# Attention between two quantised feed-forward blocks, one core: the reciprocal of the row sums moves ahead of other VectorE and GpSimd work, its spreading product one step later on TensorE

## The chip, the cores and the metric

The kernel runs on one core of a Trainium2 chip. The metric is the device time of one execution in microseconds. A core has TensorE (PE, matmuls, with its weight loads shown as PEld), VectorE (DVE), ScalarE (ACT), GpSimd (POOL) and SyncE (SP), which here only issues DMAs. Each engine works its own instruction list in order, and the lists meet in semaphores.

## The reference

```python
# x: (16, 512, 128); 16 heads of 64; all float32
x = x + 0.5 * ffn(layernorm(x))            # ffn: blockwise FP4-rounded inputs and weights, silu(gate) * up
x = x + attn(layernorm(x))
x = x + 0.5 * ffn(layernorm(x))

def attn(x):
    q, k, v = split_heads(x @ w_q), split_heads(x @ w_k), split_heads(x @ w_v)
    p = softmax(einsum('bnqd,bnkd->bnqk', q, k) * 64 ** -0.5)
    o = merge_heads(einsum('bnqk,bnkd->bnqd', p, v))
    y = o @ w_proj + b_proj + x
    return (y - mean(y)) * rsqrt(var(y) + 1e-6) * ln_gamma + ln_beta
```

## The kernel before

The program has three stages that follow one another: a feed-forward block (names with F), the attention, and the second feed-forward block (names with L). Only the attention is touched.

The attention works through NP = 128 pairs of heads, 8 pairs (PAIRS) in each of B = 16 batches. `steps(eng, body)` writes out, for each engine, the same sequence of bodies: two that fill the pipeline, the eight of batch 0, a hardware loop `Fori` over batches 1 to 14 whose one pass holds two batches (16 bodies), the eight of batch 15, and three that drain it. Body i (i = 8 b + p) has KT = 4 steps, s = 0 to 3. The order within a body is written out by hand, separately for every engine, and work of different pairs stands in one body:

- Scores of pair i, key block s: TensorE forms them transposed in two PSUM banks pS (line 956), one for each head, as three products of split operands (QH, QL, KH, KL: rounded high part and remainder) and one (SH, onesr) that subtracts the row maxima. ScalarE takes the exponential into E (line 854). POOL adds the four E of a head up in ES (lines 827 and 832). TensorE multiplies E by V into pO (line 982), one step behind the scores.
- Row maxima of the pairs i + 1 and i + 2: products pX (line 967), negated maxima on VectorE (line 902), a transposition into pR (line 1046, step 2), and SH on VectorE (line 927).
- Q and K of pair i + 2: products into pM (line 941) at the end of steps 0 and 1; QH and KH on ScalarE (861, 864), QL and KL on VectorE (919, 923). V for a later group of pairs: product at the end of step 3, copy VA on ScalarE (876).
- Row sums of pair i - 1: TensorE sums ES over the partitions into pR (line 992, step 3), ScalarE copies to LROW (871). SP spreads LROW over the partitions into LC with two DMAs (787).
- Reciprocal of pair i - 2: VectorE takes it from LC into REC, 128 x 8 (line 933, end of step 2). POOL splits REC into a high part RC[0] (line 821, step 3, ahead of the ES additions) and a remainder RC[1] (line 835, step 3, behind them). SP gathers RC into four rows of RROW with four DMAs of 2 KB (782).
- Normalisation of pair i - 3: TensorE multiplies RROW by the constant sel into pR (line 1033, end of step 0), which spreads each head's reciprocals over its 64 partitions. VectorE multiplies OT, the copied pO, by it into ON (916, step 0). The projection adds ON times wp to pY (1004, step 2); at p = 3 a product of Y and the identity comes first (1001), and at p = 2 of the next batch ScalarE copies the finished pY out (867).

So the reciprocals of a pair pass LROW, a DMA, LC, VectorE, POOL, four DMAs, RROW and TensorE. The PSUM bank pR serves three products in turn, and waits on s_norm, s_sh and s_lrow keep them apart. POOL also splits the next batch's input in the body p = 1 (801, 805). A body's SP list is: wait for s_rlo (the remainder), four row DMAs, wait for s_lrow, two DMAs of LC.

Of the kernel before, what the change touches and what calls it, by code (L numbers as in the profile page):

```python
# [11 lines left out]
F32 = mybir.dt.float32  # L12
F32R = mybir.dt.float32r
ALU = mybir.AluOpType
# [6 lines left out]
NP = B * PAIRS  # L21
# [43 lines left out]
def there(n, count):  # L65

    return not isinstance(n, int) or 0 <= n < count


def wait(eng, sem, count):  # L70

    if not isinstance(count, int) or count > 0:
        eng.wait_ge(sem, count)
# [585 lines left out]
def attention(nc, wqk, wv, w_proj, ident, xhT, Y):  # L659
    v, a, g, pe_ = nc.vector, nc.scalar, nc.gpsimd, nc.tensor  # L660
# [37 lines left out]
    with ExitStack() as scope:  # L698
# [15 lines left out]
        OT = [m.sb(f"OT{i}", [128, S]) for i in range(4)]  # L714
        ON = m.sb("ON", [128, S])
        LROW = m.sb("LROW", [128, S])
        LC = [m.sb(f"LC{i}", [128, 2, 4]) for i in range(2)]
# [50 lines left out]
        with nc.Block() as block:  # L768
# [21 lines left out]
            @block.gpsimd  # L790
            def _(pool):
                g.memset(ones[:, :], 1.0).then_inc(s_one, 1)
                pool.wait_ge(s_one, 1)

                def cols(b):

                    return xhT[:, b * S:(b + 1) * S] if isinstance(b, int) else xhT[:, bass.ds(b * S, S)]

                def split_hi(b, i):

                    g.tensor_tensor(xc[i][:, 0, :], cols(b), ones[:, 0:1].broadcast_to([128, S]), ALU.mult).then_inc(s_xhi, 1)

                def split_lo(b, i):

                    g.tensor_tensor(xc[i][:, 1, :], cols(b), xc[i][:, 0, :].bitcast(F32), ALU.subtract).then_inc(s_xc, 1)

                split_hi(0, 0)
                pool.wait_ge(s_xhi, 1)
                split_lo(0, 0)

                def body(b, p, bpar):
                    i = PAIRS * b + p
                    par = p % 2
                    for s in range(KT):
                        if s == 0 and p == 1 and there(b + 1, B) and there(b, B):
                            wait(pool, s_va, i + 3)
                        if s == 2 and p == 1 and there(b + 1, B) and there(b, B):
                            pool.wait_ge(s_xhi, b + 2)
                        if s == 3 and there(i - 2, NP):
                            pool.wait_ge(s_rec, i - 1)  # L820
                            g.tensor_tensor(RC[par][:, 0, :, :], REC[par][:, :, :],
                                            ones[:, 0:8].rearrange("p (h t) -> p h t", h=2), ALU.mult).then_inc(s_rhi, 1)
                        if s == 1 and there(i, NP):
                            pool.wait_ge(s_exp, 8 * i + 4)
                            wait(pool, s_l, i - 1)
                            for hd in range(2):
                                g.tensor_tensor(ES[par][hd][:, :], E[0][hd][:, :], E[1][hd][:, :], ALU.add).then_inc(s_add, 1)  # L827
                        if s in (2, 3) and there(i, NP):
                            pool.wait_ge(s_exp, 8 * i + 2 * s + 2)
                            for hd in range(2):  # L830
                                pool.wait_ge(s_add, 6 * i + 2 * s - 3 + hd)
                                g.tensor_tensor(ES[par][hd][:, :], ES[par][hd][:, :], E[s][hd][:, :], ALU.add).then_inc(s_add, 1)  # L832
                        if s == 3 and there(i - 2, NP):
                            pool.wait_ge(s_rhi, i - 1)
                            g.tensor_tensor(RC[par][:, 1, :, :], REC[par][:, :, :], RC[par][:, 0, :, :].bitcast(F32),
                                            ALU.subtract).then_inc(s_rlo, 1)
                        if s == 1 and p == 1 and there(b + 1, B) and there(b, B):
                            split_hi(b + 1, 1 - bpar)
                        if s == 2 and p == 1 and there(b + 1, B) and there(b, B):
                            split_lo(b + 1, 1 - bpar)  # L840
                steps(pool, body)
# [37 lines left out]
            @block.vector  # L879
            def _(dve):  # L880
                for i in range(2):
                    v.memset(SH[i][:, :].bitcast(F32), 0.0)
                v.memset(RROW[:, :].bitcast(F32), 0.0)
                v.memset(nmax[:, :], 0.0)
                v.memset(onesr[:, :].bitcast(F32), 1.0).then_inc(s_ones, 1)
                v.memset(sel[:, :].bitcast(F32), 0.0).then_inc(s_zero, 1)
                v.tensor_tensor(mask[:, :], ident[:, 0:KT], ident[:, 64:64 + KT], ALU.add).then_inc(s_ones, 1)
                dve.wait_ge(s_zero, 1)
                for hd in range(2):
                    v.tensor_tensor(sel[0:4, half(hd)], ident[0:4, hd:hd + 1].broadcast_to([4, 64]),  # L890
                                    ident[0:4, 2 + hd:3 + hd].broadcast_to([4, 64]), ALU.add).then_inc(s_ones, 1)
                dve.wait_ge(s_ones, 4)
                v.memset(LROW[:, :], 1.0).then_inc(s_ones, 1)

                def maxima(x, t):

                    if there(x, NP):
                        dve.wait_ge(s_xs, 4 * x + t + 1)
                        if t == 0:
                            wait(dve, s_mrow, x)  # L900
                        for hd in range(2):
                            v.tensor_reduce(nmax[:, 64 * hd + t:64 * hd + t + 1], pX[hd][:, :], AX.X, ALU.max,  # L902
                                            negate=True).then_inc(s_max, 1)

                def body(b, p, bpar):
                    i = PAIRS * b + p
                    par = p % 2
                    for s in range(KT):
                        if s < 2:
                            maxima(i + 1, s + 2)  # L910
                        else:
                            maxima(i + 2, s - 2)
                        if s == 0 and there(i - 3, NP):
                            dve.wait_ge(s_rb, i - 2)
                            wait(dve, s_proj, i - 3)
                            v.tensor_tensor(ON[:, :], OT[(p - 3) % 4][:, :], pR[:, :], ALU.mult).then_inc(s_norm, 1)  # L916
                        if s == 0 and there(i + 2, NP):
                            dve.wait_ge(s_qhi, i + 3)
                            v.scalar_tensor_tensor(QL[(p + 2) % 4][:, :], pM[:, :], SCALE, QH[(p + 2) % 4][:, :].bitcast(F32),  # L919
                                                   ALU.mult, ALU.subtract).then_inc(s_qlo, 1)  # L920
                        if s == 1 and there(i + 2, NP):
                            dve.wait_ge(s_khi, i + 3)
                            v.scalar_tensor_tensor(KL[(p + 2) % 4][:, :], pM[:, :], 1.0, KH[(p + 2) % 4][:, :].bitcast(F32),  # L923
                                                   ALU.mult, ALU.subtract).then_inc(s_klo, 1)
                        if s == 2 and there(i + 1, NP):
                            dve.wait_ge(s_mrow, i + 2)
                            v.tensor_tensor(SH[1 - par][0:68, :].rearrange("p (t q) -> p t q", t=KT),
                                            pR[0:68, 0:128].rearrange("p (o q) -> p o q", o=1).broadcast_to([68, KT, 128]),
                                            mask[0:68, :].rearrange("p (t o) -> p t o", o=1).broadcast_to([68, KT, 128]),
                                            ALU.mult).then_inc(s_sh, 1)  # L930
                        if s == 2 and there(i - 2, NP):
                            dve.wait_ge(s_lc, 32 * (i - 1))
                            v.reciprocal(REC[par][:, :, :], LC[par][:, :, :]).then_inc(s_rec, 1)
                steps(dve, body)

            @block.tensor
            def _(pe):
# [74 lines left out]
                def body(b, p, bpar):  # L1012
# [4 lines left out]
                    for s in range(KT):  # L1017
# [9 lines left out]
                            times_v(i, p, s - 1)  # L1027
                        if s == 3 and there(i - 1, NP):
                            row_sums(i - 1, 1 - p % 2)
                        if s == 0 and there(i - 3, NP):  # L1030
                            pe.wait_ge(s_rrow, 64 * (i - 2))
                            pe.wait_ge(s_lrow, min(i - 1, NP) if isinstance(i, int) else i - 1)
                            pe_.matmul(pR[:, :], sel[:, :], RROW[:, :], start=True, stop=True).then_inc(s_rb, 1)  # L1033
# [47 lines left out]
```

## Time and profile before

| | |
|---|---|
| Time, median of 3 runs | 3089.62 us (3083.85 to 3095.61) |
| Profiled execution | 3096.16 us, span 3094.4 us |
| TensorE busy (matmuls) | 2483.0 us, 80% |
| VectorE busy | 1587.0 us, 51% |
| POOL busy | 1408.8 us, 46% |
| ScalarE busy | 1284.9 us, 42% |
| Mean granted TensorE clock | 0.892 |

The attention stage runs from about 350 to 2742 us of the span. Busy times are sums over one profiled execution; a busy TensorE is not TensorE at its peak, since the ends of matmuls are modelled. The granted clock is 1.00 at 2.4 GHz and 0.50 at 1.2 GHz; a stretch between has parts of both.

### The profile page before, as it was taken

The page shows a single profiled execution, that of the slowest core. Times are in us where ns is not written, and L with a number is a line of the kernel's source. Part 1 is how long each engine was busy: PE and PEld are TensorE (multiplying, and loading weights), DVE is VectorE, ACT ScalarE, POOL GpSimd, SP SyncE. Part 2 cuts the span into 40 slices and gives each one's busy share as a digit, 9 for nine tenths or more (in the row PEclk, how much of TensorE's full clock was granted, in tenths as well). Part 3 has the DMA queues.
Part 4 walks back from the last instruction along what each step waited for, and adds up shares of the span by engine and source line. Part 5 has one row for each costly group of instructions (what it writes and reads, how often), then busy time and mean ns, then how long its engine had stood idle before and what let it go on. Part 6 is the DMA issues. An engine that isn't in the chain of part 4 may idle for free. (4 is left out here: it accounts for less than half of the span.)

```text
span 3094.4 us, 38590 instructions
## 1 busy us (share of the span) xinstructions
PE 2483.0 (80%) x12073; PEld 1317.5 (43%) x12073; DVE 1587.0 (51%) x2806; ACT 1284.9 (42%) x2363; POOL 1408.8 (46%) x1268
## 2 busy tenths in 40 slices
PE   4677688888888888888888888888888888846776
PEld 2455444444444444444444444444444444424444
DVE  6888544444444444444444444444444444339996
ACT  3555344343334333434334344443443444325553
POOL 3666355444445444444444444444454444435554
PEclk9877699898889888999999899999998999868778
DMA  3000000000000000000000000000000000000010
GB/s 108 28 27 20 17 1 1 2 2 2 2 1 1 1 2 1 2 1 2 1 1 2 2 2 1 2 1 1 1 2 1 2 1 2 1 18 24 21 30 17
DMA packets 143530, 27.70 MB, mean 9 GB/s; under 512 B 112064, under 2 KB 138880, under 8 KB 143360
## 3 DMA queue, kind: packets, MB, share of 16 engines
q1 hardware_dynamic: 143360, 25.43, 4.4%
q8 instruction: 107, 1.75, 0.2%
q14 instruction: 63, 0.52, 0.1%
HBM read 15.42 MB, written 8.39 MB: 8 GB/s over the span
## 5 line engine op out<-in xcount | busy, mean ns | idle before, releaser
L902 DVE TENSOR_REDUCE nmax<-pX 128x1 f32<-128x512 f32 x1024 | 659.3, 686 | 654.7 <-PE pX L967 476.5
L827 POOL TENSOR_TENSOR ES<-E 128x512 f32<-128x512 f32 x256 | 323.6, 1286 | 1087.6 <-ACT E L854 1087.6
L854 ACT ACTIVATE E<-pS 128x512 f32<-128x512 f32 x1024 | 555.9, 594 | 620.6 <-PE pS L956 614.0
L832 POOL TENSOR_TENSOR ES<-ES,E 128x512 f32<-128x512 f32 x512 | 644.8, 1281 | 238.4 <-ACT E L854 236.0
L982 PE MATMUL pO<-E,VA 128*64 128x512 f32 x2048 | 588.0, 654 | 0.0
L1033 PE MATMUL pR<-RROW,sel 128*128 128x512 f32 x128 | 78.0, 610 | 342.1 <-DMA RROW<-RC 341.3
L916 DVE TENSOR_TENSOR ON<-OT,pR 128x512 f32<-128x512 f32 x128 | 87.9, 687 | 405.5 <-PE pR L1033 405.5
L956 PE MATMUL pS<-QH,KH 64*128 64x512 f32 x1024 | 275.7, 535 | 7.2 <-issue 7.2
L941 PE MATMUL pM<-xc,wqk 128*128 128x512 f32 x768 | 266.8, 461 | 7.3 <-DMA wp<-in_L_attn_w_proj 5.2
L861 ACT ACTIVATE QH<-pM 128x512 fp32r<-128x512 f32 x128 | 76.6, 598 | 441.4 <-PE pM L941 441.4
L941 PEld LDWEIGHTS pM<-xc,wqk 128*128 128x128 f32 x768 | 155.6, 217 | 164.9 <-issue 133.9
L967 PE MATMUL pX<-KH,QH 64*128 64x512 f32 x1024 | 218.0, 419 | 5.2 <-DVE nmax L902 3.8
L1033 PEld LDWEIGHTS pR<-RROW,sel 128*128 128x128 f32 x128 | 28.2, 221 | 454.7 <-DMA RROW<-RC 409.7
L956 PE MATMUL pS<-QL,KH 64*128 64x512 f32 x1024 | 218.9, 423 | 0.0
L956 PE MATMUL pS<-QH,KL 64*128 64x512 f32 x1024 | 218.4, 421 | 0.0
L956 PE MATMUL pS<-SH,onesr 64*128 64x512 f32 x1024 | 215.9, 416 | 0.0
L982 PEld LDWEIGHTS pO<-E,VA 128*64 128x64 f32 x2048 | 106.1, 141 | 199.0 <-issue 198.7
L923 DVE SCALAR_TENSOR_TENSOR KL<-pM,KH 128x512 fp32r<-128x512 f32 x128 | 88.5, 691 | 193.9 <-ACT KH L864 193.9
L956 PEld LDWEIGHTS pS<-QH,KH 64*128 64x128 f32 x1024 | 102.2, 196 | 181.1 <-issue 164.0
L919 DVE SCALAR_TENSOR_TENSOR QL<-pM,QH 128x512 fp32r<-128x512 f32 x128 | 88.5, 692 | 112.4 <-ACT QH L861 112.4
L864 ACT ACTIVATE KH<-pM 128x512 fp32r<-128x512 f32 x128 | 76.7, 599 | 164.7 <-PE pM L941 164.7
L1004 PE MATMUL pY<-wp,ON 128*128 128x128 f32 x1024 | 137.5, 278 | 2.3 <-DVE ON L916 2.3
(156 smaller groups left out, 3565.2 us busy)
## 6 DMA issues: line engine op xcount, KB each, us to landing
RROW<-RC SPq DMA_DIRECT2D x512, 2.0 KB, 2.0
Fxin<-in_L_attn_x SPq DMA_DIRECT2D x16, 256.0 KB, 2.8
Y<-in_L_attn_x SPq DMA_DIRECT2D x16, 256.0 KB, 5.0
x<-Fxout SPq DMA_DIRECT2D x16, 256.0 KB, 2.0
LC<-LROW SPq DMA_DIRECT2D x256, 2.0 KB, 2.1
Lx1in<-x SPq DMA_DIRECT2D x16, 256.0 KB, 2.7
out<-Lxout SPq DMA_DIRECT2D x16, 256.0 KB, 2.9
w_raw<-in_L_attn_w_q SPq DMA_DIRECT2D x1, 512.0 KB, 5.6
```

Of the source, the lines that this page charges most:

```text
L827: g.tensor_tensor(ES[par][hd][:, :], E[0][hd][:, :], E[1][hd][:, :], ALU.add).then_inc(s_add, 1)
L832: g.tensor_tensor(ES[par][hd][:, :], ES[par][hd][:, :], E[s][hd][:, :], ALU.add).then_inc(s_add, 1)
L854: a.activation(E[s][hd][:, :], pS[hd][:, :], ACT.Exp).then_inc(s_exp, 1)
L902: v.tensor_reduce(nmax[:, 64 * hd + t:64 * hd + t + 1], pX[hd][:, :], AX.X, ALU.max, negate=True).then_inc(s_max, 1)
L919: v.scalar_tensor_tensor(QL[(p + 2) % 4][:, :], pM[:, :], SCALE, QH[(p + 2) % 4][:, :].bitcast(F32), ALU.mult, ALU.subtract).then_inc(s_ql ...
L923: v.scalar_tensor_tensor(KL[(p + 2) % 4][:, :], pM[:, :], 1.0, KH[(p + 2) % 4][:, :].bitcast(F32), ALU.mult, ALU.subtract).then_inc(s_klo, 1)
L941: ins = pe_.matmul(out, w[k], x[l], start=n == 0, stop=n == 2)
L956: ins = pe_.matmul(pS[hd][:, :], lhs, qq[half(hd), :], start=n == 0, stop=n == 3)
L967: ins = pe_.matmul(pX[hd][:, :], QH[f][half(hd), t * 128:t * 128 + 128], KH[f][half(hd), :], start=True, stop=True)
L982: ins = pe_.matmul(pO[half(hd), :], VA[of][:, kt, j * 128 + 64 * hd:j * 128 + 64 * hd + 64], E[kt][hd][:, :], start=kt == 0, stop=kt == KT ...
L1004: ins = pe_.matmul(pY[:, t * 128:(t + 1) * 128], ON[:, t * 128:(t + 1) * 128], wp[:, po, :], start=False, stop=po == PAIRS - 1 and t == T - 1)
L1033: pe_.matmul(pR[:, :], sel[:, :], RROW[:, :], start=True, stop=True).then_inc(s_rb, 1)
```

## The change

The reciprocal (line 933) moves from the end of step 2 to step 1 on VectorE, behind ON and ahead of KL. Both operations of its split (821, 835) move from step 3 to the start of step 2 on POOL, ahead of that step's ES additions. The spreading product (1033) moves from the end of step 0 to the end of step 1 on TensorE, ahead of the K product, and ON (916) moves from step 0 to step 1 on VectorE. SP's list is as it was, and so is every operand.

```diff
@@ POOL
-                        if s == 3 and there(i - 2, NP):
+                        if s == 2 and there(i - 2, NP):
                             pool.wait_ge(s_rec, i - 1)
                             g.tensor_tensor(RC[par][:, 0, :, :], REC[par][:, :, :],
                                             ones[:, 0:8].rearrange("p (h t) -> p h t", h=2), ALU.mult).then_inc(s_rhi, 1)
+                            pool.wait_ge(s_rhi, i - 1)
+                            g.tensor_tensor(RC[par][:, 1, :, :], REC[par][:, :, :], RC[par][:, 0, :, :].bitcast(F32),
+                                            ALU.subtract).then_inc(s_rlo, 1)
...
-                        if s == 3 and there(i - 2, NP):
-                            pool.wait_ge(s_rhi, i - 1)
-                            g.tensor_tensor(RC[par][:, 1, :, :], REC[par][:, :, :], RC[par][:, 0, :, :].bitcast(F32),
-                                            ALU.subtract).then_inc(s_rlo, 1)
@@ VectorE
-                        if s == 0 and there(i - 3, NP):
-                            dve.wait_ge(s_rb, i - 2)
-                            wait(dve, s_proj, i - 3)
-                            v.tensor_tensor(ON[:, :], OT[(p - 3) % 4][:, :], pR[:, :], ALU.mult).then_inc(s_norm, 1)
                         if s == 0 and there(i + 2, NP):
                             dve.wait_ge(s_qhi, i + 3)
                             v.scalar_tensor_tensor(QL[(p + 2) % 4][:, :], pM[:, :], SCALE, QH[(p + 2) % 4][:, :].bitcast(F32),
                                                    ALU.mult, ALU.subtract).then_inc(s_qlo, 1)
+                        if s == 1 and there(i - 3, NP):
+                            dve.wait_ge(s_rb, i - 2)
+                            wait(dve, s_proj, i - 3)
+                            v.tensor_tensor(ON[:, :], OT[(p - 3) % 4][:, :], pR[:, :], ALU.mult).then_inc(s_norm, 1)
+                        if s == 1 and there(i - 2, NP):
+                            dve.wait_ge(s_lc, 32 * (i - 1))
+                            v.reciprocal(REC[par][:, :, :], LC[par][:, :, :]).then_inc(s_rec, 1)
...
-                        if s == 2 and there(i - 2, NP):
-                            dve.wait_ge(s_lc, 32 * (i - 1))
-                            v.reciprocal(REC[par][:, :, :], LC[par][:, :, :]).then_inc(s_rec, 1)
@@ TensorE
-                        if s == 0 and there(i - 3, NP):
+                        if s == 1 and there(i - 3, NP):
                             pe.wait_ge(s_rrow, 64 * (i - 2))
                             pe.wait_ge(s_lrow, min(i - 1, NP) if isinstance(i, int) else i - 1)
                             pe_.matmul(pR[:, :], sel[:, :], RROW[:, :], start=True, stop=True).then_inc(s_rb, 1)
```

## Rows read from the trace of the kernel before

**Rows 1.** The page's groups of instructions, two rows (busy, mean ns | idle before, releaser).
```profile
L1033 PE MATMUL pR<-RROW,sel 128*128 128x512 f32 x128 | 78.0, 610 | 342.1 <-DMA RROW<-RC 341.3
...
L941 PE MATMUL pM<-xc,wqk 128*128 128x512 f32 x768 | 266.8, 461 | 7.3 <-DMA wp<-in_L_attn_w_proj 5.2
```

**Rows 2.** Busy time by stretch, first to 125th spreading product (header row first).
```profile
core 0: us, PE busy (x) PEld busy (x) DVE busy (x) ACT busy (x) POOL busy (x), PEclk, DMA share, GB/s
...
426.20:2707.20 2281.00, 1944.47 (x9808) 964.18 (x9808) 977.71 (x1604) 913.96 (x1622) 1008.73 (x1020) 0.93 0.03 2
```

**Rows 3.** Timeline of one body (start us, duration us, engine, line, xcount [idle before, releaser]).
```profile
1513.03 0.19 DVE L933 RECIPROCAL REC<-LC 128x8 f32<-128x8 f32 x1
...
1514.50 2.53 POOL L832 TENSOR_TENSOR ES<-ES,E 128x512 f32<-128x512 f32 x2 [0.75 <-ACT E L854]
...
1515.35 0.59 ACT L871 ACTIVATE LROW<-pR 65x512 f32<-65x512 f32 x1 [1.01 <-PE pR L992]
...
1516.05 0.19 PEld L956 LDWEIGHTS pS<-QH,KH 64*128 64x128 f32 x2 [0.36 <-issue]
...
1516.98 0.21 POOL L835 TENSOR_TENSOR RC<-REC,RC 128x8 fp32r<-128x8 f32 x1
...
1517.22 2.45 SPq L782 DMA_DIRECT2D RROW<-RC  x4
...
1521.09 0.80 PE L1033 MATMUL pR<-RROW,sel 128*128 128x512 f32 x1 [2.60 <-DMA RROW<-RC]
```

**Rows 4.** The page's DMA issues (xcount, KB each, median us from issue to landing).
```profile
RROW<-RC SPq DMA_DIRECT2D x512, 2.0 KB, 2.0
```

**Rows 5.** Line 787 (LC<-LROW), its landings.
```profile
DMA to landing us min/median/max: 2.0/2.1/3.5
```

**Rows 6.** Busy time by stretch after a stall, and later in that body.
```profile
1501.23:1507.52 6.29, 6.29 (x19) 2.94 (x19) 2.67 (x4) 1.68 (x3) 0.87 (x1) 0.51 0.02 1
1508.42:1518.50 10.08, 10.07 (x59) 4.99 (x58) 4.95 (x9) 5.02 (x9) 6.12 (x7) 1.00 0.01 1
```

**Rows 7.** Timeline, starts of the spreading product: the first four, and one at 1501.
```profile
426.21 0.50 PE L1033 MATMUL pR<-RROW,sel 128*128 128x512 f32 x1 [2.14 <-DMA RROW<-RC]
...
443.96 0.50 PE L1033 MATMUL pR<-RROW,sel 128*128 128x512 f32 x1 [2.44 <-DMA RROW<-RC]
...
460.87 0.50 PE L1033 MATMUL pR<-RROW,sel 128*128 128x512 f32 x1 [2.43 <-DMA RROW<-RC]
...
477.86 0.50 PE L1033 MATMUL pR<-RROW,sel 128*128 128x512 f32 x1 [2.50 <-DMA RROW<-RC]
...
1501.23 0.80 PE L1033 MATMUL pR<-RROW,sel 128*128 128x512 f32 x1 [2.58 <-DMA RROW<-RC]
```

**Rows 8.** Timeline of body 2, which has no spreading product and no projection.
```profile
407.77 0.50 PE L956 MATMUL pS<-QH,KH 64*128 64x512 f32 x2
...
413.40 0.97 PE L941 MATMUL pM<-xc,wqk 128*128 128x512 f32 x3
413.44 2.54 POOL L827 TENSOR_TENSOR ES<-E 128x512 f32<-128x512 f32 x2 [3.96 <-ACT E L854]
...
414.41 0.60 ACT L864 ACTIVATE KH<-pM 128x512 fp32r<-128x512 f32 x1 [1.04 <-PE pM L941]
...
415.33 0.40 PE L967 MATMUL pX<-KH,QH 64*128 64x512 f32 x2
415.54 1.08 ACT L854 ACTIVATE E<-pS 128x512 f32<-128x512 f32 x2 [0.53 <-PE pS L956]
...
416.67 0.33 PE L1046 MATMUL pR<-ident,nmax 128*128 128x128 f32 x1
...
421.63 0.50 PE L956 MATMUL pS<-QH,KH 64*128 64x512 f32 x2
```

**Rows 9.** Timeline, first scores after a jump of the loop.
```profile
1702.95 0.50 PE L956 MATMUL pS<-QH,KH 64*128 64x512 f32 x2 [1.16 <-issue]
```

**Rows 10.** Timeline, spreading products of the last body and the first draining one.
```profile
2707.18 0.80 PE L1033 MATMUL pR<-RROW,sel 128*128 128x512 f32 x1 [3.77 <-DMA RROW<-RC]
...
2724.21 0.80 PE L1033 MATMUL pR<-RROW,sel 128*128 128x512 f32 x1 [5.03 <-DMA RROW<-RC]
```

## The prediction

> **What bounds the kernel now.** I read the page's groups first. The product that spreads the reciprocals over the lanes (pR<-RROW,sel) has 342.1 us of idle TensorE before it, released by the DMA of RROW; the next of the matmul groups has 7.3 us [rows 1]. So in the attention stage TensorE sets the pace and waits for one thing. The stretch from the first to the 125th of these products, 426 to 2707 us, is 2281 us of the 3094.4 us span; TensorE is busy in 1944 us of it, at a mean granted clock of 0.93 [rows 2]. The timeline of one body (one head pair) shows the loop. The reciprocal runs on VectorE at 1513.03, 0.19 us. Its high part follows on POOL; the low part stands behind two ES additions (1514.50, 2.53 us) and comes at 1516.98. Only then does SP issue the four row DMAs, 1517.22, 2.45 us of issuing, and the product starts at 1521.09 after 2.60 us without work [rows 3]. One DMA lands 2.0 us after issue [rows 4], and the last of four is issued 0.6 us before the 2.45 end, so 1517.22 + 2.45 - 0.6 + 2.0 = 1521.1: the wait is that chain and nothing else.
>
> The stall costs twice. At 1501.23 it is followed by 6.29 us at a granted clock of 0.51, the 1.2 GHz level; 1508.42 to 1518.50 ran at 1.00, 2.4 GHz [rows 6]. The starts of the product show both prices: 16.99 us a body where the clock stays up (460.87 to 477.86), 19.86 where it fell after the stall (1501.23 to 1521.09), against 2281 / 124 = 18.40 on average [rows 2, 3, 7].
>
> **The change, part by part.** Nothing is added or removed: 128 reciprocals, 256 small POOL operations, 512 row DMAs and 128 products stay. Only places shift. I let a body start (t = 0) with its first score product at full clock. The offsets below are those of body 2, which ran without a stall, from 407.77 [rows 8], plus 0.3 us behind the product's new place (my estimate from a third of the K product's 0.97 us for three of the same size).
>
> *The product, one step later.* It moves from the end of step 0 to the end of step 1, ahead of the K product at 413.40, so to t = 5.6 [rows 8]. Its pR bank must be free (the LROW copy is done before t = 0: 1515.35 + 0.59, with the body at 1516.05 [rows 3]), and ON must be done before the transposition takes the bank: ON ends at 5.6 + 0.5 + 0.7 = 6.9, the transposition comes at 416.67, so 8.9 + 0.3 = 9.2. Cost nothing. TensorE's order puts Q ahead of it then, and QH and QL come 0.3 us earlier.
>
> *The reciprocal*, from the end of step 2 to step 1 behind ON: 6.9 to 7.1. It needs LC, which SP issues after LROW and which lands 2.1 us later [rows 5]. No row DMAs stand ahead of it any more, so 1.2 us of issue and 2.1 of flight from t = 0 put LC there at about 3.2. Behind the reciprocal on VectorE waits KL, which waits for KH anyway until about 7.6 (KH starts at 414.41, takes 0.60: 6.64 + 0.60 + 0.3). Cover 0.5 us; 0.19 us of KL if it were gone.
>
> *The split on POOL*, from step 3 to the start of step 2, both halves together. ES of step 1 runs 5.7 to 8.2 (413.44, 2.54), the halves follow to 8.65 (2 x 0.20 and a gap), and the addition of step 2 has its exponentials only at about 9.2 (415.54 + 1.08) [rows 8]. Cost nothing. In the one body in eight that also splits the next batch's input, the split stands about one more addition later, 1.3 us by its half in the row at 1514.50 [rows 3]; the slack of the rows (below) swallows that.
>
> *The row DMAs* follow on SP at 8.9 and are down by 8.9 + 2.45 + 1.4 = 12.8. The product that needs them stands at 14.5 + 5.6 = 20.1. Slack 7 us: the stall goes whole.
>
> **What is late next.** By these times nothing. The tightest wait I find is pX of step 2 for KH: KH ends at 7.6, pX is due at 415.33, so 7.9 [rows 8]; it is the same order as before and it holds in bodies that ran without the stall. Another comes once in 16 bodies, where the loop jumps: there TensorE idles 1.16 us for "issue" (1702.95), now partly hidden since the row DMAs run on meanwhile [rows 9]. It will stand bare, 6 or 7 times.
>
> **The sum.** A body without stall at full clock: 16.99 - 2.50 = 14.49, 16.91 - 2.43 = 14.48, so 14.47 [rows 3, 7]; body 2 took 13.86 (407.77 to 421.63) [rows 8], and the product (0.3) and a projection (0.9) less what TensorE there idled and lost behind the missing projection (0.6, an estimate) bring that to the same. One body in eight adds the copy of Y into pY: 17.75 - 2.44 = 15.31, so 0.85 more [rows 7]. For 124 bodies: 124 x 14.47 + 16 x 0.85 + 7 x 1.15 for the jumps - 4.4 for the last bodies, which lack the V or Q and K products = 1811 us. Before they took 2281: 470 us less. Of this about 329 are stall (342.1 less some 13 before the first product and in the tail [rows 1]) and 141 clock. Then the tail: the last body's stall of 3.77 us and some 1.8 us of low clock behind it go (2707.18) [rows 10]. Past the last exponential the chain of two reciprocals, their row DMAs and LC remains, but RROW of pair 125 is already there, so the 5.03 us before 2724.21 shrink; I redo the chain with the durations of before (ES 2.5, row sums 1.0, LROW 0.6, LC 3.3, reciprocal and split 0.9, rows 4.0, product, ON, projection, copy 3.7) and get 4.3 us less [rows 10]. Together 470 + 9 = 479 (the parts of the tail overlap by a microsecond). The profiled execution took 3096.16, so 2617 us; it stands 6.5 us above the median, so 2611 for the median.
>
> A rule weighed. By the granted clock alone, 2281 us at 0.93 [rows 2] are 319 us at the low level. The Trainium skill, TensorE: Matmul & The Clock Gate, section "HAM oscillation", prices such time at its length times (1 - K/N), here one half. That would be 160 us instead of my 141 and would put the kernel at 2592. The rows say slightly less than half: without their stalls the body from 1501.23 took 17.26 us and the one from 460.87 took 14.49, so 2.8 us for 6.29 us at the low clock [rows 3, 6, 7]. I stay with the rows.
>
> **Rivals.**
> 1. *The stall goes, the clock does not come back.* If the low stretches had another cause than the idle time, only the 329 + 9 come back: 3090 - 338 = 2752. For: the clock fell after some stalls and not after others of the same 2.6 us. Against: the low stretches begin in or right after a stall, and 407.8 to 421.6 without one ran on at full pace, 13.86 us [rows 8]. 4%.
> 2. *A new wait takes part of the place.* pX behind KH has 0.25 us; VectorE now goes pR, ON, reciprocal, KL in one step. If a step loses 0.3 to 0.7 us in each body, that is 128 x 0.5 = 64 us: 2675. For: small margins. Against: every arrival above is worked out from rows of the same order. 8%.
> 3. *Slower.* VectorE works in order, and the reciprocal now stands ahead of KL and all later maxima. If LC arrived late, VectorE would stop there, then SH, then the scores. The stop starts to bite at 7.1 + 0.5 = 7.6 and reaches TensorE when the maxima of step 2 (due at 9.2) slip, so with LC later than about 8.3. It makes the kernel slower than before when each body loses more than 479 / 128 = 3.7 us, LC at 12 or later; say 5 us a body: 3090 - 479 + 640 = 3251. For: the wait is new in that place. Against: the slowest LC landing in the trace is 3.5 us [rows 5], which gives 4.7. 2%.
> 4. *It does nothing*, because the product still ends up behind the same DMA: 3090. It would need the rows to land 7 us later than they do. 1%.
>
> **Chances and range.** Forecast 85%, the rest as above. The forecast's own range is 2590 (0.17 us a body less: body 2 with only 0.4 added) to 2650 (0.3 us a body more). The range given reaches into rival 2: 2588 to 2690. No difference under 0.5% (15 us) can be told from no change here; faster takes the forecast and rivals 1 and 2, 97%, same 1%, slower 2%.
>
> **What would show it.** Idle before the product of pR near zero, from 342; 14.5 us from one product to the next in nearly all bodies; granted clock 1.00 through the attention stage; the four row DMAs issued 7 us before the product starts; VectorE's idle time before the reciprocal still a few us in total. I am wrong if the clock stays at 0.93 without stalls, if pX or the scores show new waits for VectorE or ScalarE, or if the time is over 2690.

## The result and the profile after

The changed kernel takes 2611.68 us (median, 2611.11 to 2615.99), against 3092.61 us for the kernel before in the same comparison: ratio 0.8447, 95% interval 0.8419 to 0.8476. The forecast was 2611 (2588 to 2690). The profiled execution took 2615.99 us, its span is 2614.2 us (before 3094.4). Line numbers moved by one: the spreading product is line 1032, pX 966, scores 955.

The groups of instructions (all groups, of the changed kernel; busy, mean ns | idle before, releaser) answer to [rows 1]:

```profile
L940 PE MATMUL pM<-xc,wqk 128*128 128x512 f32 x768 | 236.9, 417 | 7.2 <-DMA wp<-in_L_attn_w_proj 5.1 <-DVE QL L914 2.1
...
L1032 PE MATMUL pR<-RROW,sel 128*128 128x512 f32 x128 | 64.9, 507 | 6.2 <-DMA RROW<-RC 6.2
...
L922 DVE RECIPROCAL REC<-LC 128x8 f32<-128x8 f32 x128 | 25.0, 195 | 1.3 <-DMA LC<-LROW 1.3
```

The 342.1 us of idle TensorE are 6.2, all of it in the two last products, and no other group of matmuls has taken them over. The reciprocal waits for LC once, 1.3 us. The stretch from the first to the 125th product answers to [rows 2] (columns as there):

```profile
428.43:2234.36 1805.93, 1797.41 (x9805) 897.39 (x9803) 976.52 (x1602) 913.35 (x1621) 1016.74 (x1020) 1.00 0.03 2
```

1805.9 us instead of 2281.0, TensorE busy in 1797, granted clock 1.00 instead of 0.93. The busy times of VectorE, ScalarE and POOL are within 1% of what they were. TensorE's 1944 us are 1797 for the same matmuls, since these no longer run at the low clock: 147 us of the 475 are the clock. The other part is the waits for RROW in this stretch, 125 of them and 331.4 us before, none after; the remaining idle time of TensorE went from 5 to 8.5 us. One body in the timeline (start us, duration us, [idle before, releaser]), from its first scores to the next spreading product but one, answers to [rows 3, 7]:

```profile
1255.48 1.17 SPq L787 DMA_DIRECT2D LC<-LROW  x2
1255.56 0.50 PE L955 MATMUL pS<-QH,KH 64*128 64x512 f32 x2
...
1261.18 0.50 PE L1032 MATMUL pR<-RROW,sel 128*128 128x512 f32 x1
1261.34 2.55 POOL L830 TENSOR_TENSOR ES<-E 128x512 f32<-128x512 f32 x2 [4.82 <-ACT E L853]
...
1261.71 0.69 DVE L919 TENSOR_TENSOR ON<-OT,pR 128x512 f32<-128x512 f32 x1
...
1262.32 0.20 DVE L922 RECIPROCAL REC<-LC 128x8 f32<-128x8 f32 x1
1262.41 0.60 ACT L863 ACTIVATE KH<-pM 128x512 fp32r<-128x512 f32 x1 [1.14 <-PE pM L940]
...
1263.04 0.69 DVE L925 SCALAR_TENSOR_TENSOR KL<-pM,KH 128x512 fp32r<-128x512 f32 x1 [0.52 <-ACT KH L863]
...
1263.34 0.40 PE L966 MATMUL pX<-KH,QH 64*128 64x512 f32 x2
...
1263.84 0.21 POOL L821 TENSOR_TENSOR RC<-REC,ones 128x8 fp32r<-128x8 f32 x1
1264.13 0.20 POOL L824 TENSOR_TENSOR RC<-REC,RC 128x8 fp32r<-128x8 f32 x1
1264.36 2.45 SPq L782 DMA_DIRECT2D RROW<-RC  x4
...
1264.68 0.33 PE L1045 MATMUL pR<-ident,nmax 128*128 128x128 f32 x1
...
1264.94 2.52 POOL L835 TENSOR_TENSOR ES<-ES,E 128x512 f32<-128x512 f32 x2 [0.61 <-ACT E L853]
...
1275.59 0.51 PE L1032 MATMUL pR<-RROW,sel 128*128 128x512 f32 x1
```

1261.18 to 1275.59 is 14.41 us. The row DMAs are issued 11.2 us before the product that reads them; with the 3.87 us that they took from first issue to the product in [rows 3] they leave 7.4 us unused. KL waits 0.52 us for KH and not for the reciprocal. The addition of step 2 still waits for its exponentials (0.61 us), so the split ahead of it cost nothing.

### The profile page after: what moved, and what is told of

Read it like the earlier page. It is cut to its first block and busy times, and to the rows that moved or that the text cites. A ratio compares the mean times of both kernels' runs of the same rounds, so it can differ in the third digit from the quotient of the medians.

```text
span 2614.2 us, 38604 instructions
## 1 busy us (share of the span) xinstructions
PE 2342.2 (90%) x12073; PEld 1253.6 (48%) x12073; DVE 1587.1 (61%) x2806; ACT 1283.8 (49%) x2363; POOL 1416.6 (54%) x1268
## 5 line engine op out<-in xcount | busy, mean ns | idle before, releaser
L981 PE MATMUL pO<-E,VA 128*64 128x512 f32 x2048 | 553.2, 618 | 0.0
L955 PE MATMUL pS<-QH,KH 64*128 64x512 f32 x1024 | 256.6, 497 | 8.5 <-issue 8.3
L940 PE MATMUL pM<-xc,wqk 128*128 128x512 f32 x768 | 236.9, 417 | 7.2 <-DMA wp<-in_L_attn_w_proj 5.1
L955 PE MATMUL pS<-QL,KH 64*128 64x512 f32 x1024 | 204.3, 395 | 0.0
L955 PE MATMUL pS<-QH,KL 64*128 64x512 f32 x1024 | 204.0, 394 | 0.0
L940 PEld LDWEIGHTS pM<-xc,wqk 128*128 128x128 f32 x768 | 135.8, 191 | 131.8 <-issue 105.3
L870 ACT ACTIVATE LROW<-pR 65x512 f32<-65x512 f32 x128 | 76.1, 595 | 132.9 <-PE pR L991 132.9
L1003 PEld LDWEIGHTS pY<-wp,ON 128*128 128x128 f32 x1024 | 133.4, 200 | 12.1 <-issue 8.5
L609 PE MATMUL LpGU<-wguT,LxqT 128*128 128x352 f32 x256 | 117.0, 613 | 17.4 <-ACT LxqT L553 11.8
L991 PE MATMUL pR<-ES,ones 128*64 128x512 f32 x512 | 131.6, 592 | 0.0
```

The costliest lines, as they stand in the source:

```text
L609: ins = pe_.matmul(pGU[:, t % 2, k, 0:FF], xqT[iH][:, t * 128:(t + 1) * 128], wguT[:, k, 0:FF], start=True, stop=True)
L940: ins = pe_.matmul(out, w[k], x[l], start=n == 0, stop=n == 2)
L955: ins = pe_.matmul(pS[hd][:, :], lhs, qq[half(hd), :], start=n == 0, stop=n == 3)
L981: ins = pe_.matmul(pO[half(hd), :], VA[of][:, kt, j * 128 + 64 * hd:j * 128 + 64 * hd + 64], E[kt][hd][:, :], start=kt == 0, stop=kt == KT ...
L991: ins = pe_.matmul(pR[half(hd), :], ones[:, 0:64], ES[par][hd][:, :], start=True, stop=True)
L1003: ins = pe_.matmul(pY[:, t * 128:(t + 1) * 128], ON[:, t * 128:(t + 1) * 128], wp[:, po, :], start=False, stop=po == PAIRS - 1 and t == T - 1)
```

## The experiments

All ran beside the kernel before, and ratios are to it. Two theories at first. S: the stall is a matter of slack in one chain, and either end of it, moved by enough, removes it whole. T: the two moves are both needed.

**1. Product and ON alone, one step later.**

```diff
-                        if s == 0 and there(i - 3, NP):    # product 1033 on TensorE, ON on VectorE
+                        if s == 1 and there(i - 3, NP):
```

> Only the spreading product and ON move one step later; reciprocal and split stay where they were. Theory S (the stall is a matter of slack: whichever end of the chain moves by enough removes it all): in the trace of before the four row DMAs are issued 1.17 us after a body's first scores and land 3.9 us later, at 5.1; the product one step later is due at 5.6. So no stall in most bodies, about 0.3 us in the one of eight whose POOL also splits the next input; granted clock near 1.00 in the attention; total 2610 to 2625 us, like the whole change. Rival T (both moves are needed): part of the stall stays, 1 us or more a body, and with it low clock: 2700 or more.

2634.92 us (2632.74 to 2640.30), ratio 0.8508 (0.8493 to 0.8523). T falls. S is right in kind and 10 us low: by the ratios, 96% of the gain is there. The waits (total us, times, longest), then the landings of the row DMAs (us from issue to landing):

```profile
PE pR L1033 <- DMA RROW<-RC: 25.2, 19, 5.0
```

```profile
DMA to landing us min/median/max: 1.9/2.0/3.9
```

Seventeen products between the first and the 125th still wait, about 1 us each (16.7 us), and they are not the bodies that I had named. This kernel has only some 0.6 us between the usual arrival of the rows and the product. In the first of these waits the rows were issued on time, and the product came 5.8 us behind the first issue instead of 3.9:

```profile
580.17 2.45 SPq L782 DMA_DIRECT2D RROW<-RC  x4
...
585.99 0.50 PE L1033 MATMUL pR<-RROW,sel 128*128 128x512 f32 x1 [1.27 <-DMA RROW<-RC]
```

So a part of the landings is up to 2 us late: 24 of the 128 groups of four row DMAs have one that took over 2.5 us, and 16 of the 17 waits stand behind such a group. The profile shows what goes with them: a 16 KB transfer of another queue, the one that it calls instruction. From the DMA queues between 580 and 587 us (packets, MB, share of 16 engines):

```profile
q8 instruction: 1, 0.02, 1.3%
```

Such a transfer overlaps all 24 late groups, and 23 of the 104 others. The whole change has landings up to 3.7 us as well (4 late groups) and waits for none. The rest of the difference is the tail: the 125th product to the last takes 27.7 us here and 20.8 in the whole change.

**2. Reciprocal and split alone, ahead.** The POOL and VectorE parts of the change, with the product and ON left in step 0.

```diff
-                        if s == 1 and there(i - 3, NP):    # the changed kernel's product and ON
+                        if s == 0 and there(i - 3, NP):
```

> Only the reciprocal and its split move ahead; the product and ON stay in step 0. Theory S: the rows land about 12.8 us after a body's first scores and the product is due at 14.4 + 2.4 = 16.8, so 4 us of slack and no stall anywhere: 2605 to 2620 us. Rival T: part of the stall stays: 2700 or more.

2609.64 us (2608.49 to 2611.71), ratio 0.8425 (0.8411 to 0.8439). No product waits outside the tail. This half gives the whole gain.

**3. One POOL operation.**

```diff
+                            pool.wait_ge(s_rhi, i - 1)     # step 3, right behind the high part
+                            g.tensor_tensor(RC[par][:, 1, :, :], REC..., RC[par][:, 0, :, :].bitcast(F32), ALU.subtract)
...
-                        if s == 3 and there(i - 2, NP):    # no longer behind the ES additions
-                            pool.wait_ge(s_rhi, i - 1)
```

> One POOL operation moves: the remainder of the split stands right behind the high part in step 3, ahead of the ES additions of that step; reciprocal, product and ON stay. Theory S: the row DMAs start at about 12.6 and land at 16.5, the product is due at 16.8: no stall in seven bodies of eight, about 1 us in the eighth, whose split of the input stands ahead on POOL: 2615 to 2650 us, most of the gain from 0.2 us of work moved by one place. Rival T: the reciprocal must move too: 2900 or more.

2642.46 us (2639.08 to 2644.78), ratio 0.8525 (0.8511 to 0.8540).

```profile
PE pR L1032 <- DMA RROW<-RC: 32.6, 31, 3.6
```

```profile
1503.61 0.20 POOL L821 TENSOR_TENSOR RC<-REC,ones 128x8 fp32r<-128x8 f32 x1
1503.89 0.20 POOL L824 TENSOR_TENSOR RC<-REC,RC 128x8 fp32r<-128x8 f32 x1
1504.12 2.45 SPq L782 DMA_DIRECT2D RROW<-RC  x4
```

The first fence is the wait, the second the timeline: in the kernel before, the remainder came 3.4 us behind the high part (1513.54 to 1516.98, the latter in [rows 3]), here it is 0.28 us. Moving 0.2 us of work past 2.5 us of other work gives 95% of the gain. One body in eight waits as expected (14 bodies, 1.1 to 1.6 us, some 18 us together). Of the rest of the 32.6 us, 8 are 14 other waits up to the 125th product, all but one behind a late landing, and 6.6 are the tail.

**4. The reciprocal alone, ahead.**

```diff
-                        if s == 2 and there(i - 2, NP):    # reciprocal on VectorE, behind SH
+                        if s == 1 and there(i - 2, NP):    # ahead of KL
```

> Only the reciprocal moves, to step 1 on VectorE; split, product and ON stay. Both theories: the remainder still stands behind the ES additions of step 3, which wait for the last exponentials, so the rows are issued when they were: stall 340 us, 3080 to 3100 us, no change. If the reciprocal were what held the chain, it would be over 100 us faster.

3098.12 us (3089.10 to 3120.01), ratio 1.0027 (0.9993 to 1.0062): no change.

```profile
PE pR L1033 <- DMA RROW<-RC: 344.9, 128, 5.0
```

The stall is all there. The reciprocal had not been late: the remainder behind it was.

**5 and 6. What the clock alone is worth.** The kernel before, its wait filled with products whose result is overwritten (ten in one kernel, five in the other).

```diff
+                        if s == 0 and there(i - 3, NP) and there(i + 2, NP):
+                            wait(pe, s_va, i + 4 if not isinstance(i, int) else min(i + 4, ROUNDS))
+                            for _ in range(10):            # 5 in the second kernel
+                                pe_.matmul(pM[:, :], sel[:, :], QH[p % 4][:, :], start=True, stop=True)
                         if s == 0 and there(i - 3, NP):
                             pe.wait_ge(s_rrow, 64 * (i - 2))
```

> The kernel before, with ten extra products of 512 columns into the free bank pM (overwritten by the Q product) ahead of the spreading product's wait: they take 10 x 0.23 = 2.3 us at the high clock and lie inside the wait of 2.6 us. The wait for the row DMAs stays as long. Theory C (the low clock comes from TensorE having no work in the stall): granted clock 1.00 in the attention, a body takes 17.0 to 17.2 us everywhere, so about 141 us less than before: 2945 to 2960 us. Rival D (the clock falls for another reason, such as the load itself): clock 0.93 or lower as before, and 3090 us or more, since the extra products cost where the clock is low.

> As the one with ten extra products, but five (1.2 us), so that about 1.4 us of the wait stay without work. Theory C: the clock falls rarely or never after so short an idle time, 2945 to 2970 us. Rival: any idle time of that sort can bring the clock down, in proportion: about half of the clock's price stays, 3010 to 3030 us.

Ten: 2984.16 us (2981.73 to 2987.41), ratio 0.9647 (0.9582 to 0.9712). Five: 3004.49 us (3003.82 to 3011.87), ratio 0.9723 (0.9657 to 0.9790). The stretch from the first to the 125th product, first with ten, then with five (PEclk is the third number from the end); the ten-product kernel's added products alone in the same stretch (TensorE, weight loads, clock); and two bodies of its timeline, one without a wait and one with:

```profile
426.83:2598.40 2171.57, 2118.23 (x11028) 1121.35 (x11027) 978.26 (x1604) 914.46 (x1622) 1009.56 (x1020) 0.99 0.03 2
```

```profile
423.43:2615.20 2191.77, 2004.40 (x10417) 1018.58 (x10417) 978.28 (x1604) 914.57 (x1622) 1009.12 (x1020) 0.98 0.03 2
```

```profile
426.83:2598.40 2171.57, 318.20 (x1221) 220.49 (x1220) 0.99 0.03 2
```

```profile
1476.28 2.59 PE L1033 MATMUL pM<-QH,sel 128*128 128x512 f32 x10
1478.95 0.50 PE L1037 MATMUL pR<-RROW,sel 128*128 128x512 f32 x1
...
1510.52 2.60 PE L1033 MATMUL pM<-QH,sel 128*128 128x512 f32 x10
1514.07 0.50 PE L1037 MATMUL pR<-RROW,sel 128*128 128x512 f32 x1 [0.95 <-DMA RROW<-RC]
```

Work that computes nothing makes the kernel 3.5% faster, since the clock stays up (0.99 against 0.93 in [rows 2]). That shows the cause: the low clock came from TensorE's idle time, not from its load. Both times lie outside what I had put down for theory C (2945 to 2960, and 2945 to 2970), and the second also misses its rival (3010 to 3030).

The ten-product kernel does not show the price of the clock by its time alone, because the filling has a price too. Ten products took 2.6 us and not 2.3, so they outlast the wait in most bodies: only 35 of the 125 products still wait. The added products (318 us) and the waits that are left (36 us) make 354 us, where the kernel before waited 331. TensorE's other idle time is some 12 us longer, 5 of it at the loop's jumps. TensorE's busy time without the added products is 1800 us (2118 - 318), 144 less than before and close to the 1797 of the changed kernel. So the clock gave back 144 us, and 35 of them were spent again: 109 us are left in the stretch. With five products 120 waits stay, 1.2 us at the median and 173 us in all; the busy time without the added ones is 1827 us (2004 - 177). That is 117 of the 147 us: the price falls with the idle time and does not vanish at half of it.

**7 and 8. A late LC.** The whole change with further DMAs of the same shape ahead of the two of LC, four in one kernel, fourteen in the other. The counts that ScalarE and VectorE wait for on s_lc are raised to match, in lines not shown here.

```diff
+                        for k in range(4):                 # 14 in the second kernel
+                            sp.dma_start(J[new][:, k, :], LROW[64 * (k % 2):64 * (k % 2) + 1, :]).then_inc(s_lc, 16)
                         for hd in range(2):
                             sp.dma_start(LC[new][:, hd, :], LROW[64 * hd:64 * hd + 1, :]).then_inc(s_lc, 16)
```

> The whole change, with four more DMAs of the same shape (LROW into a scratch tile) issued ahead of the two of LC, so LC lands 4 x 0.6 = 2.4 us later, at about 5.5 after a body's first scores; VectorE reaches the reciprocal at 6.9. Theory L (a late LC costs nothing until the reciprocal's own place, then it holds VectorE, the maxima of step 2 and TensorE behind them): no effect, 2608 to 2620 us. Rival M (more DMAs in the body cost by themselves, by SP's issuing or by later landings of the row DMAs): 2640 us or more.

> As the one with four, but fourteen: LC lands 8.4 us later, at about 11.4, which is 4.5 us past the place of the reciprocal. Theory L: the maxima of step 2 (start 9.3 before) start at 12.3, the product pX of step 3 waits about 2.2 us for them in each body: 2611 + 126 x 2.2 = 2890 us, 2830 to 2960, more if the clock falls; the idle time stands before pX or the row sums, released by VectorE. Rival N (VectorE's later work has slack enough, as it is busy half of the time): under 2700.

Four: 2617.38 us (2615.43 to 2620.32), ratio 0.8459 (0.8406 to 0.8512). No product waits before the tail, whose last two bodies are 5 us longer. Rival M (2640 or more) falls. Fourteen: 3027.16 us (3023.22 and 3031.11), ratio 0.9780 (0.9699 to 0.9860), beyond the range of theory L. Its waits and its timeline:

```profile
DVE REC L925 <- DMA LC<-LROW: 640.2, 128, 9.0
...
PE pX L969 <- DVE nmax L904: 275.1, 127, 4.0
...
PE pR L1035 <- DMA RROW<-RC: 27.8, 3, 11.5
```

```profile
1506.72 0.20 DVE L925 RECIPROCAL REC<-LC 128x8 f32<-128x8 f32 x1 [4.72 <-DMA LC<-LROW]
1506.84 0.64 DVE L928 SCALAR_TENSOR_TENSOR KL<-pM,KH 128x512 fp32r<-128x512 f32 x1
...
1507.39 1.28 DVE L904 TENSOR_REDUCE nmax<-pX 128x1 f32<-128x512 f32 x2
...
1508.73 0.50 PE L969 MATMUL pX<-KH,QH 64*128 64x512 f32 x2 [2.10 <-DVE nmax L904]
```

```profile
430.00:2600.00 2170.00, 1898.28 (x9715) 911.64 (x9716) 953.23 (x1590) 905.35 (x1606) 993.18 (x1006) 0.96 0.08 3
```

The mechanism is theory L's: 4.72 us at the reciprocal, then maxima, then 2.10 us on TensorE where I had 2.2. What the range left out ("more if the clock falls") is the clock, 0.96 again in the last fence (430 to 2600). From the first to the 125th product this kernel takes 2194.7 us, 389 more than the whole change: 268 of them are waits of pX, and 120 are longer busy times of TensorE (1917 against 1797 us). The tail is 24 us longer. The rival of the prediction that ended slower is real in mechanism, then, but starts late: 2.4 us of delay cost nothing in the bodies, 8.4 us give 86% of the gain back.

**9 to 11. Which version is best.** On one chip: reciprocal and split alone (as 2), the whole change, and the first of these with the attention's loop written out.

```diff
-        with eng.Fori(0, B // 2 - 1) as c:
+        for c in range(B // 2 - 1):
```

> Reciprocal and split ahead, product and ON in step 0 (as in the earlier run with this edit), now beside the whole change on the same chip. Theory: the two differ by 0.03 us a body (14.39 against 14.42 in the traces), 3 to 5 us in all: 2605 to 2612 us, same as the whole change within 0.3%.

> The whole change once more, for the comparison on one chip: 2608 to 2618 us.

> As the kernel with only reciprocal and split ahead, with the attention's hardware loop written out (no jumps, every wait a constant). Theory: the six bodies at the jumps took 15.5 to 15.9 us instead of 14.4, so 8 us go: 2598 to 2604 us, 0.3% faster. Rival: the straight code must be fetched too and costs as much or more: 2610 us or more.

2609.05 us (2608.31 to 2610.74), 2611.21 us (2607.68 to 2613.45) and 2599.68 us (2597.05 to 2600.55); ratios 0.8432 (0.8396 to 0.8469), 0.8438 (0.8401 to 0.8475), 0.8402 (0.8365 to 0.8438). The first two are the same for practical purposes, and the executions of the third all lie below those of both. In the changed kernel TensorE idles at a jump as here (the longest body of the six; behind it part of the body ran at the low clock):

```profile
1664.85 0.50 PE L955 MATMUL pS<-QH,KH 64*128 64x512 f32 x2 [1.70 <-issue]
```

The version with the loop written out and the product left in step 0 beats both kernels of this study.

## Why the prediction was right

*What bounds the kernel.* One chain held TensorE. Experiment 4 narrows this: the link that was late was the remainder of the split behind two ES additions, and experiments 1 to 3 show that any of three edits removes almost all of the stall.

*The places.* Counted from the first scores at 1255.56: product 5.6 (predicted 5.6), reciprocal 6.8 (6.9), end of the split 8.8 (8.65), row DMAs 8.8 (8.9), transposition 9.1 (9.2), next product 20.0 (20.1), slack 7.4 (7). KL waits 0.52 us for KH (0.5). pX stands 0.33 us behind the end of KH (0.25 to 0.3).

*The sum.* A body: 14.42 us (14.47). The stretch of 124 bodies: 1805.9 us (1811), so 475 us less (470). The tail: 20.8 us from the 125th product to the last instead of 30.5, 9.7 less (9). The jumps: six bodies of 15.6 to 17.8 us, 10 us above the others (8). The parts before and after the stretch differ by 2 us each. Spans: 480 us less (479).

*Stall and clock.* The sum split the 470 us of the stretch in 329 for the stall and 141 for the clock. The traces bear out both terms: the waits were 331 us and went to nothing, and the busy time of TensorE fell by 147 us for the same matmuls; some 3 us more of other idle time leave 475. Experiment 5 agrees with 144 us. The time of experiment 5, 109 us less in the stretch, is not that price but what is left of it after the filling has been paid for. Its range was wrong in this: it took ten products for 2.3 us and let them lie inside the wait.

*The luck in it.* That the forecast meets the median within 1 us is chance. The stretch saved 5 us more than summed, and the parts before and after it took 4.5 us more, which the sum left out.

*The rule weighed.* The Trainium skill (TensorE: Matmul & The Clock Gate, "HAM oscillation") would have given an estimate of 160 us for the clock. My rows gave 141, and the busy times show 147, nearer to the rows. The estimate by this rule of the Trainium skill is no sharper than the clock read into it: 0.93 is rounded, and 0.925 to 0.935 make it 171 to 148 us. That an idle wait for a DMA brings the half rate each time it comes, as the page of the Trainium skill tells of its example with waits of about 3 to 5 us, this trace does not show for its shorter ones. Of 77 waits between 2.58 and 2.62 us in the kernel before, 40 have low clock in the wait or in the 7 us behind it, and 37 have none.

*The rivals.* The first (clock not regained) is refuted by the clock of 1.00 and by experiment 5. The second (new waits of 0.3 to 0.7 us) did not come. The third needed LC at 12 us after the first scores to make the kernel slower than before; experiment 8 put it at about 11.6 (the reciprocal at 1506.72; its body began at 1495.1, 5.6 us ahead of the spreading product at 1500.77) and came to 0.978 of before. My 3.7 us of loss in each body as the break-even holds only if the clock is counted in: a body lost 3.1 us there, 2.2 waiting and 1.0 by the clock. A kernel slower than before was not measured.

## What to carry to other kernels

Where an engine waits once in each turn for a long chain over other engines and DMAs, work out the arrival of each link against the turn, and look for the small operation that stands behind large ones on an in-order engine: here 0.2 us of POOL work, moved by one place, gave 95% of a gain of 480 us. Count a wait on TensorE twice, once for its length and once for the clock that it loses in the work behind it: 331 and 147 us here. To read the second part, compare TensorE's busy time over the same matmuls. And give a chain that ends in DMAs more slack than their median time: 0.6 us left one product in seven waiting, 7 us none.

## What the hardware showed beside that

- The row DMAs land in 2.0 us at the median. The slowest of 512 took 3.7 to 3.9 us in four of these kernels (the whole change, experiments 1, 3 and 8) and 2.9 in the kernel before. Over the thirteen profiled executions 133 of 1664 groups of four have a landing over 2.5 us. A 16 KB transfer of the instruction queue overlaps every one of them, and 176 of the other 1531. So the late landings have that transfer in common; that it delays them was not tested, and why it delays some groups and not others stays open.
- A jump of the loop costs TensorE more in some passes than in others: 1.2 to 3.3 us in the changed kernel, up to 5.6 us with ten more products in each body, in the longest of them with some low clock. Without the loop all six are gone, and the straight code cost nothing that shows.
- With waits of 1.2 us at the median in nearly every body the mean clock of the stretch was 0.98, with 2.6 us 0.93, without any 1.00.
